# Expert weights before the tile three places ahead, in each step of the first stage

## What is computed

```python
y   = einsum('bsi,boi->bso', x, weight[itok])             # 128 x 64 x 1024, 16 experts
h   = einsum('bsd,nrd->nbsr', y, lora_A)
out = x + einsum('bsd,od->bso', y, W) + bias \
        + einsum('nbsr,nor->bso', h, lora_B * (2 * lora_weights)[:, None, None])
```

## Time and profile before

| | |
|---|---|
| median of 3 runs | 1505.84 us (1505.27 to 1507.7) |
| profiled execution, its own time | 1505.41 us |
| its span (first to last instruction) | 1503.7 us |
| TensorE busy in the span | 1489.9 us, 99% |
| VectorE, ScalarE, GpSimd busy | 788.1, 393.4, 464.3 us |

### The profile page before, as it was taken

How to read it: one execution, slowest core, us unless ns; L and a number is a source line. 1 busy time by engine, 2 the same in 40 slices (tenths; PEclk the granted TensorE clock), 3 DMA queues, 4 the chain that set the end, 5 groups by cost and what they waited for, 6 DMA issues and landing times.

```text
span 1503.7 us, 29749 instructions
## 1 busy us (share of the span) xinstructions
PE 1489.9 (99%) x6354; PEld 1189.6 (79%) x6355; DVE 788.1 (52%) x1192; ACT 393.4 (26%) x493; POOL 464.3 (31%) x651
## 2 busy tenths in 40 slices
PE   7999999999999999999999999999999999999998
PEld 4878888888888888878888888888888888888887
DVE  8857776467777467478843333333333333333331
ACT  5334443244443243244431111111111111111110
POOL 4365533443433443433102221212212212212111
PEclk9999999999999999999999999999999999999999
DMA  9978876667777467479645455555555555554553
GB/s 280 296 216 241 219 207 156 180 182 210 205 216 200 140 188 197 145 199 234 187 148 141 134 146 140 138 141 143 141 135 141 146 140 136 148 140 134 145 140 84
DMA packets 172705, 257.90 MB, mean 172 GB/s; under 512 B 31616, under 2 KB 135552, under 8 KB 172672
## 3 DMA queue, kind: packets, MB, share of 16 engines
q1 hardware_dynamic: 128896, 138.62, 35.6%
q10 hardware_dynamic: 23360, 73.28, 16.3%
q0 software_dynamic: 20416, 45.65, 10.7%
HBM read 181.93 MB, written 75.50 MB: 171 GB/s over the span
## 4 chain that ended last, share of the span: by engine, by line
PE 94%; DMA 2%; SPq 2%; DVE 1%; issue 1%; ACT 0%; DVEq 0%; ACTq 0%
PE ps L758 31%; PE ps L765 31%; PE ps L762 31%; DMA w_place<-in_L_cond_weight_dram 2%; SPq L208 1%; SPq L230 1%; DVE w_turn L537 0%; DVE w_lo L593 0%; SPq L197 0%; ACT x_hi L415 0%; PE ps L786 0%; DVE x_turn L624 0%; SPq L215 0%; ACT w_hi L407 0%; DVE x_lo L631 0%
## 5 line engine op out<-in xcount | busy, mean ns | idle before, releaser
L758 PE MATMUL ps<-w_hi,x_hi 128*128 (+1 forms) x2096 | 531.7, 395 | 2.5 <-ACT x_hi L415 1.2
L762 PE MATMUL ps<-w_hi,x_lo 128*128 (+1 forms) x2096 | 531.3, 395 | 0.0
L765 PE MATMUL ps<-w_lo,x_hi 128*128 (+1 forms) x2096 | 531.3, 395 | 0.0
L758 PEld LDWEIGHTS ps<-w_hi,x_hi 128*128 128x128 f32 x2096 | 392.4, 187 | 100.8 <-issue 3.1
L762 PEld LDWEIGHTS ps<-w_hi,x_lo 128*128 128x128 f32 x2096 | 392.7, 187 | 96.4
L765 PEld LDWEIGHTS ps<-w_lo,x_hi 128*128 128x128 f32 x2096 | 392.7, 187 | 96.4
L208 POOL DMA_DIRECT2D x_raw<-in_x_dram x560 | 299.1, 534 | 407.8 <-DVE x_turn L624 240.7
L624 DVE STREAM_TRANSPOSE x_turn<-x_raw 128x256 f32<-128x256 f32 x544 | 193.7, 414 | 440.7 <-DMA x_raw<-y_scr 380.5
L415 ACT ACTIVATE x_hi<-x_turn 128x512 fp32r<-128x512 f32 x272 | 167.4, 630 | 690.6 <-DVE x_turn L624 676.4
L390 POOL TENSOR_TENSOR stage<-stage,w_place 128x1024 f32<-128x1024 f32 x64 | 153.0, 2390 | 610.2 <-DMA stage<-in_x_dram 610.2
L631 DVE TENSOR_TENSOR x_lo<-x_turn,x_hi 128x512 fp32r<-128x512 f32 x272 | 180.6, 691 | 121.2 <-ACT x_hi L415 116.1
(11 more groups left out here) (71 smaller groups left out, 39.7 us busy)
## 6 DMA issues: line engine op xcount, KB each, us to landing
w_place<-in_L_cond_weight_dram SPq DMA_DIRECT2D x480, 128.0 KB, 4.5
y_scr<-stage ACTq DMA_DIRECT2D x72, 512.0 KB, 4.2
x_raw<-in_x_dram POOLq DMA_DIRECT2D x560, 64.0 KB, 3.8
x_raw<-y_scr SPq DMA_DIRECT2D x512, 64.0 KB, 2.4
stage<-in_x_dram SPq DMA_DIRECT2D x128, 256.0 KB, 3.7
out_dram<-stage ACTq DMA_DIRECT2D x126, 256.0 KB, 3.0
weff<-fold_sb POOLq DMA_DIRECT2D x8, 512.0 KB, 12.3
w_place<-weff SPq DMA_DIRECT2D x32, 128.0 KB, 3.2
```

What stands on the lines that cost most here:

```text
L758: mm(ps[b][:, cols], x_hi[b][:, t, :], hi[t], start=t == 0, stop=False)
L762: mm(ps[b][:, cols], x_lo[b][:, t, :], hi[t], start=False, stop=False)
L765: last = mm(ps[b][:, cols], x_hi[b][:, t, :], lo[t], start=False, stop=t == KT - 1)
```

## The change

In the step of a slot, VectorE and ScalarE each look at the table and prepare the next expert's matrix first, and x(s+3) after it. This holds for all slots of the first stage, in the written-out first and last slots as in the loops. Nothing is added or removed, and the other engines' lists are the same.

```diff
@@ ScalarE
             for slot in range(1, RING):
+                round_next_expert(slot)
                 if slot > 1:
                     round_x(slot + AHEAD, (slot + AHEAD) % RING)
-                round_next_expert(slot)
                 move_y(slot, slot, 0)
             with act.Fori(1, SLOTS // RING) as g:
                 for u in range(RING):
                     slot = g * RING + u
+                    round_next_expert(slot)
                     round_x(slot + AHEAD, (u + AHEAD) % RING)
-                    round_next_expert(slot)
                     move_y(slot, u, g)
@@ VectorE
             for slot in range(1, RING):
                 n = slot + AHEAD
+                prepare_next_expert(slot)
                 if slot > 1:
                     prepare_x(n, n % RING, n % RING, x_index(n))
-                prepare_next_expert(slot)
             with dve.Fori(1, SLOTS // RING - 1) as g:
                 for u in range(RING):
                     slot = g * RING + u
                     v = u + AHEAD
+                    prepare_next_expert(slot)
                     prepare_x(slot + AHEAD, v % RING, v % RING, g + x_index(v))
-                    prepare_next_expert(slot)
             for u in range(RING):
                 slot = SLOTS - RING + u
                 n = slot + AHEAD
+                prepare_next_expert(slot)
                 if n < SLOTS:
                     prepare_x(n, n % RING, n % RING, x_index(n))
                 else:
                     prepare_x(n, n % RING, n % RING, (n - SLOTS) // RING, [y_loaded], 2 * QUADS)
-                prepare_next_expert(slot)
```

## The result

| | before | after |
|---|---|---|
| median, lowest to highest of 5 runs each | 1505.84 us (1505.13 to 1507.7) | 1514.68 us (1513.7 to 1515.08) |
| ratio, 95% interval | | 1.0057 [1.0042, 1.0071] |
| profiled execution, and its span | 1505.41, 1503.7 us | 1514.91, 1513.3 us |

What follows compares the result with a forecast made beforehand. TensorE, busy 1489.9 of 1503.7 us, was taken as the bound. 5.4 (wait) + 1.7 (clock) + 0 = 7.1 us on 1505.41 gave 1512.5, plus 0.43 to the median: 1512.9 us, range 1509.9 to 1516.5.

Steps and rivals of the forecast that it cites:

- first rival: Ahead of tile 9: TensorE waits 5.4 us but its clock holds or returns at once, 1511.2 us; chance 0.20.
- third and fourth: Not slower, x(9) in time in slot 6, 1505.8 or 1504.4 us; or the change doesn't act; together 0.07.
- Slot 6, the matrix: VectorE in slot 6: the matrix of rank 2 follows x(8) directly and starts at 103.4, 4.4 us earlier.
- second rival: Ahead of tile 9: wait lengthened by late chunks or table reads, 1516 us, 1519 at the far end; chance 0.15.
- Slot 6, x(9): Ahead of tile 9: x(9) turned at 123.5, first half rounded at 124.9, so TensorE idles 5.4 us.
- a loss there would be swallowed: Any delay at tile 6 vanishes in tile 9's wait, whose end VectorE sets, not TensorE.
- Steps 1 to 3: Slots that open nothing: only a table read moves ahead of x(5) and x(6); taken as 0, upper end 0.6 us.
- No other wait over 0.5 us: Expected sign: apart from the gap ahead of tile 9, TensorE has no new wait over 0.5 us.
- The clock: After the wait at tile 9 TensorE runs at half clock for a while: 1.7 us, between 0 and 3.5.
- Slots 7 and on: After slot 6: x(10), y(6) and the load of x(13) shift but stay in time; one stall, no chain.
- the other openings: Later slots that open an expert, from 11 on: margins of 4.8 to 8.5 us, so no stall.
- Late loads: Slot 6, matrix chunks 4 to 7 asked for 4.4 us earlier: taken as 0, other end 4.4 us.

Runs made afterwards that it cites:

- step 6 alone: The kernel before with slots 4 to 7 written out and the new order in slot 6 only: 1514.91 us, ratio 1.0055.
- the first eight experiments: All follow-up kernels but the two that move y(2) first: new order in some slots, the control, cut matrix, extra matmuls; medians 1505.90 to 1514.91 us.
- the two with y(2) moved first: ScalarE moves y(2) ahead of rounding x(5), with new order in slots 1 to 3 only: 1506.42 us; in the kernel before: 1505.94 us.
- the two part kernels: The kernel before with the new order in slots 1 to 3 only, 1509.03 us, and in slot 6 only, 1514.91 us.
- the changed kernel without steps 4 to 7: The changed kernel with slots 4 to 7 written out in the old order: 1507.94 us, ratio 1.0008.
- steps 1 to 3 alone: The kernel before with the new order only in written-out slots 1 to 3, where no expert opens: 1509.03 us, ratio 1.0014.
- sixteen matmuls: The changed kernel with 16 thrown-away matmuls of 512 columns ahead of tile 9 to keep TensorE busy: 1512.97 us, ratio 1.0047.

## Why the prediction was right, and where its steps were off

**The place and the mechanism held.** The wait stands ahead of tile 9, ended by the rounding of x(9), and step 6 alone gives the whole loss. The first rival fell, since the clock did not hold; the third and fourth fell by the time. No chunk of the matrix came late: no gap of VectorE inside it is put down to a DMA.

**Slot 6, the matrix: right, but 1.5 us late.** Its first chunk was turned at 104.90, not 103.4. x(8) ended at 103.8 instead of 102.33, since its loads came later. GpSimd's timeline, to read against the earlier trace rows:

```profile
87.48 1.16 POOL L208 DMA_DIRECT2D x_raw<-in_x_dram  x2 [1.86 <-issue]
...
91.95 2.38 POOL L208 DMA_DIRECT2D x_raw<-in_x_dram  x4 [2.09 <-issue]
```

They were issued 1.04 and 1.14 us later; a longer table read stands in GpSimd's list ahead of them. The view of line 197 from 80 to 88 us, before and then after:

```profile
L197 POOLq TENSOR_LOAD <-slot_tab x2: 286/490/694, 81.5 to 84.7; - x2
```

```profile
L197 POOLq TENSOR_LOAD <-slot_tab x2: 287/752/1217, 82.0 to 85.2; - x2
```

This is mostly the execution's chance: over before, after and the first eight experiments x(8) was turned at 99.03 to 100.94 in the five kernels with the old order in steps 1 to 3, and at 99.60 to 100.98 in the five with the new; it was 98.03 and 96.87 in the two with y(2) moved first. The prediction took one execution's 99.50 for fixed, and its own list of signs has x(8) landing at another time as one of being wrong; in this part it was. Of the second rival, a longer wait by late chunks or table reads, the table read is the part that came.

**Slot 6, x(9): the term of 5.4 us was 7.3.** With the matrix 0.3 us longer (20.38 instead of 20.07; ScalarE came 0.67 us late for its first chunk), x(9) was turned at 125.28, not 123.5, and tile 9 started 7.33 us later than before. Only 3.88 us of this stand in the trace as idle time there, since TensorE had already lost 3.3 us at tile 6. The prediction's statement that a loss there would be swallowed is what the two part kernels show.

**Steps 1 to 3: taken as 0, with 0.6 as the end; it was 1.7 us, and 3.3 with the clock.** The step that failed is its reading of the table reads as a delay of x(6) alone, 0.6 us. They delay x(5) by 1.20 us, behind it y(2)'s move, and behind that TensorE's own table reads, of which the longest took 1.40 us. "No other wait over 0.5 us" was wrong by this. It cost the sum nothing.

**The clock: 1.7 us taken, 2.6 measured** in the profiled execution, 1.8 with step 6 alone (140.16 less 127.20, less 11.20), inside the 0 to 3.5 of the text. That the clock would fall in such a wait was right; how long it stays low behind it was not. The term took 3.4 us of half clock after the restart (its own rows, 7.5 to 11, give 3.5); in the changed kernel it stood at half from 125.7 until 132.5, 5.6 us of it behind tile 9's start at 126.89. The reading of the run's start rests on the rate of the matmuls alone: the trace gives a granted clock of 1.00 for every stretch from 0 to 16 us.

**Slots 7 and on, and the other openings: 0 expected, 0 found.** GpSimd's load of x(13) went out at 127.51 instead of 121.64, and nobody waited for it; the changed kernel without steps 4 to 7 has no wait after tile 6. **Late loads: 0 expected, 0 found.**

The sum on the profiled executions was 7.1 us and is 9.5: 1.9 more of wait and 0.9 more of clock, less 0.4 that came back between tile 10 and tile 70. Between the medians it is 8.8, since the profiled execution of after lies 0.2 us above its median and that of before 0.4 below.

## What to carry to other kernels

Where an engine runs ahead of a full TensorE, list how long each tile is ready before its need, and set the length of the block that is moved ahead of it against that: with a margin of 14.0 us a move by 10.4 us cost no wait, one by 14.8 cost 0.8 us and one by 21.6 cost 7.6, and fourteen other openings, whose margins in the changed kernel were 5.6 us and more, cost nothing. A loss ahead of a wait that another engine ends is not added to it, so time an edit's parts apart before summing them. Count in a move also the small things that stand in a step, a table read or a move out of PSUM, up to the one that the full engine's own list waits for.

## What the runs showed of the hardware that was not expected

**The clock falls after shorter waits than the end of the run suggested.** TensorE's clock fell from 2.4 to 1.2 GHz after idle times of 1.82, 2.28, 2.42, 2.44 and 2.59 us, in five executions, and held after 1.15, 1.43 and 1.71 us in others. Nor does it fall only inside the wait: with steps 1 to 3 alone TensorE started tile 6 at 87.39, and the clock was full until 88.7. In runs of that one kernel it fell in six of eleven, by their times. One fall costs 1.3 to 2.6 us (a tile of 12.57 to 13.84 us); behind the waits of 1.8 to 2.6 us that is half to nine tenths of the wait itself, so a short stall next to a full TensorE has to be priced at up to 1.9 times its length where the clock may fall.

The cost is about half of the stretch at half clock that lies behind the restart, not a matter of the wait's length. For tile 9, clock back at 132.5 after a start at 126.89 cost 2.6 us (wait 3.88); back at 130.9 after 127.20 cost 1.8 (step 6 alone, wait 6.72); back at 129.4 after 125.93 cost 1.6 (sixteen matmuls, wait 2.28). The longest wait was not the dearest, since the clock had fallen at 124.1, 3.1 us before its end.

The Trainium skill (TensorE: Matmul & The Clock Gate, What's actually happening) says that the number of slow matmuls at a kernel's start varies between runs of the same kernel. It speaks of the start; in the middle of this one the runs agree so far as the clock falls in some of them and not in others.

**A sequencer's read of a small table has no fixed price.** Reads of the slot table at line 197 took 0.26 to 1.45 us between 80 and 88 us of the traced executions. On GpSimd and on TensorE such a read stands on the path to a load or to a tile. Whether it is behind the run-to-run spread of this stage was not tested.
